# Cross-attention and a mixture-of-experts feed-forward on one core: setup and first turns reordered, biases added at read-out, feed-forward from the middle of turn 2

## The chip, the cores and the metric

One core of one Trainium2 chip runs the whole program. The metric is the device time of one execution, in microseconds (us), as the median of several runs. The engines are TensorE (PE in the profile; its weight loads are PEld), VectorE (DVE), ScalarE (ACT), GpSimd (POOL) and SyncE (SP), whose queue issues the DMAs.

## What is computed

`x`, `fside` (here `ctx1`) and `ctx_1024` (here `ctx2`) have the shape (16, 256, 256): 16 batches of 256 tokens of width 256. Everything is float32.

```
x1 = x + attention(layernorm(x), ctx1, memory = ctx2)
     q = ln(x) Wq + bq;  k = ctx1 Wk + bk;  v = ctx1 Wv + bv
     k, v = concat([k, ctx2]), concat([v, ctx2])        # 512 keys
     16 heads of 16;  softmax(q k^T / 4) v;  then Wp + bp
out = x1 + sum over 8 experts e of  cw_e * (silu(z Wg_e) * (z Wu_e)) Wd_e
     z = layernorm(x1);  F = 1024
     cw = softmax(z w_router) * softmax(10 z w_gating), normalised over e
```

## The kernel before, in words

Precision. A float32 operand is split into a high part (rounded to the fp32r format) and a low part (the rest), and a product is three matmuls: high x high, high x low, low x high (`passes`). The high part is written by ScalarE (or VectorE for the attention weights), the low part by VectorE (`h_lo`, `xT_lo`, `cT_lo`) or GpSimd (`wg_lo`, `kstack`, `qstack`).

Turns and steps. The order of work is written out by hand. One turn handles one batch's attention and has 32 steps; in step i the scores of item i+8 (`ps_s`, L714), their maximum (`negmax`, L1092, VectorE), the transposed scores (`ps_t`, L723), the exponential (`Pt`, L870, ScalarE), its low part (`Pt_lo`, L1039 on VectorE for i % 8 in 1, 3, 5, 7, else L1182 on GpSimd) and, six steps behind, the product with V (L694, L696) are done, each engine walking the same list of steps. Two turns ahead of turn 0 (-2 and -1) hold the setup of the first batches. `turn.has(d)` says whether batch b+d exists, and `turn.wait` waits on a counter.

The list `MISC` (L279) names further TensorE items by step: cT and xT (transposes of the context and of the normalised x), kv, q and o (projections; `project`, L504, q and o in two halves over two steps), kT (transposes of the key stack), qq (of the maxima and the query stack), aT, x2T, lg and cwT (transpose of the attention result, transpose of z, router logits, transpose of the combine weights), and y (output transposes of a finished group). ScalarE or VectorE reads each item's bank in the same step. Before the feed-forward the items, the scores and the transposed scores alternate between two PSUM banks; from then on each has one bank (`one_bank`, `bank`).

Biases. `project` begins with a matmul of `minus_one` by `brow` (L507), which puts the bias in PSUM; brow is made in the setup.

Feed-forward. A group is two batches (512 tokens), 8 experts, 8 steps each of 128 hidden columns: 64 steps a group, 512 in all, one for each attention step. A step f has six gate matmuls (L617, ps_s), six up matmuls (L617, ps_t) and six down matmuls (L651), each of 512 columns; ScalarE takes tanh (L737) and the high part (L742), VectorE the products L904 and L911 and the low part L916. At the last step of an expert VectorE weighs the output (two L931) and GpSimd adds it (L1140). It starts at turn `LAG` = 3, step 0; `before_ffn` and `first_weights` prepare the first step and the first weights in one piece, ahead of turn 3 and ahead of turn 1. Turns 3 to 15 are joint (attention and feed-forward); after turn 15's attention the rest of the feed-forward runs alone.

Setup. SP issues Wq, Wk, Wv, Wp, the router's two parts, four bias rows and the first three expert weights, and then X and C1 of batch 0 (L411, L414). VectorE waits for the first ten of these, splits all weights, clears tiles and makes brow; TensorE waits for all of it (`const_ready`, `w_split`) before its first instruction.

Of the kernel before, what the change touches and what calls it, by code (L numbers as in the profile page):

```python
# [21 lines left out]
ALU = mybir.AluOpType  # L22
# [14 lines left out]
def bass_xattn_moe_ffn_kernel(nc, x, ctx1, ctx2, Wq, bq, Wk, bk, Wv, bv, Wp, bp, w_router, w_gating,  # L37
# [28 lines left out]
    LAG = GB + 1  # L66
# [8 lines left out]
    FTURNS = FSTEPS // STEPS  # L75
    assert FTURNS == GB * GROUPS
# [12 lines left out]
    with ExitStack() as ctx:  # L89
# [11 lines left out]
        with ExitStack() as early:  # L101
            def raw(name, shape, dt=F32):
                return early.enter_context(nc.sbuf_tensor(name, shape, dt))

            wraw = raw("wraw", [P, 4, DC, D])
            rraw = raw("rraw", [P, DC, 2 * E])
            braw, bhi = raw("braw", [2, 4, D]), raw("bhi", [2, 4, D], F32R)
# [11 lines left out]
        brow = sb("brow", [P, 4, D], F32R)  # L119
        minus_one = sb("minus_one", [P, P], F32R)  # L120
# [6 lines left out]
        XN = sb("XN", [P, QT, D])  # L127
        C1 = sb("C1", [P, QT, D])
# [3 lines left out]
        QK = sb("QK", [P, QT, D])  # L132
        VF = sb("VF", [P, KC, D])
# [68 lines left out]
        w_in = sem("w_in"); const_ready = sem("const_ready"); w_split = sem("w_split")  # L202
        x_in = Count("x_in", 16); c1_in = Count("c1_in", 16); c2_in = Count("c2_in", 16)
        xr_in = Count("xr_in", 16)
# [8 lines left out]
        kv_ps = Count("kv_ps", 2); k_done = Count("k_done", 2); v_done = Count("v_done", 2)  # L213
# [24 lines left out]
        CONSTS = 13  # L238
        W_PARTS = 13
        LAST = LAG + FTURNS  # L240

        class Turn:


            def __init__(self, b):
                self.b, self.ffn = b, LAG <= b
                self.closed = (b - LAG) // GB - 1 if self.ffn and (b - LAG) % GB == 0 and b > LAG else None
# [22 lines left out]
        def turns(body, before_ffn=None, first_weights=None):  # L270

            for b in range(-2, LAST + 1):
                if b == 1 and first_weights:
                    first_weights()
                if b == LAG and before_ffn:
                    before_ffn()
                body(Turn(b))

        MISC = [(0, "kT", 5, 0), (1, "kT", 6, 0), (2, "qq", 1, 0), (3, "cT", 0, 1), (4, "kT", 7, 0), (5, "y", 0, 0),  # L279
# [9 lines left out]
        def released(turn, name, k, d):  # L289

            if name == "y":
                return [] if turn.closed is None else [(y_done, turn.closed * GB + k + 1)]
            if name == "qq":
                ahead, da = q_ahead(k, d)
                freed = [(d, qm_done, 2 * k + 2), (da, qT_done, 2 * ahead + 2)]
                return [(count.sem, (turn.b + at) * count.per + nth) for at, count, nth in freed if turn.has(at)]
            count, nth = {"kT": (kT_done, k + 1), "kv": (v_done, k + 1), "xT": (xT_l, 1), "cT": (cT_l, 1), "aT": (aT_l, 1),
                          "x2T": (x2T_l, 1), "q": (q_done, 1), "o": (x1_done, 1), "lg": (ldif_done, 1),
                          "cwT": (cwT_done, 1)}[name]
            return [(count.sem, (turn.b + d) * count.per + nth)] if turn.has(d) else []  # L300

        def misc(turn, step):

            for n, (s, name, k, d) in enumerate(MISC):
                if s == step and released(turn, name, k, d):
                    return n, name, k, d
            return None, None, None, None

        def second_half(turn, step):

            n, name, _, d = misc(turn, step - 1)
            return (n, name) if name in ("q", "o") else (None, None)

        def one_bank(turn, banks, i):

            return banks[0] if turn.ffn else banks[i % 2]

        def octet_bank(turn, o):

            return ps_a[:] if turn.ffn or o % 2 else ps_o[:, 0, :]  # L320

        def wait_read_out(eng, turn, count, d, i):

            turn.wait(eng, count, d, i if turn.ffn else i - 1)

        ORDER = [sum(item[1] != "y" for item in MISC[:n]) for n in range(len(MISC))]

        def bank(turn, n):

            return ps_o[:, 1, :] if ORDER[n] % 2 and not turn.ffn else ps_m[:]  # L330

        def wait_bank(eng, turn, n):

            same = [m for m in range(len(MISC)) if turn.ffn or MISC[m][1] != "y" and (ORDER[m] - ORDER[n]) % 2 == 0]
            earlier = [(Turn(turn.b - 1), m) for m in same] + [(turn, m) for m in same if m < n]
            for then, m in reversed(earlier):
                freed = released(then, *MISC[m][1:])
                for counter, value in freed:
                    eng.wait_ge(counter, value)
                if freed:  # L340
                    return
# [7 lines left out]
        V_AT = ((3, 5, 0), (0, 14, 1), (1, 22, 1), (2, 30, 1))  # L349
# [42 lines left out]
        def _(eng):  # L392
            for n, w in enumerate((Wq, Wk, Wv, Wp)):
# [848 lines left out]
```

## Time and profile before

| | |
|---|---|
| median of 3 runs | 2844.45 us (2843.43 to 2844.73) |
| profiled execution | 2842.41 us, span 2840.6 us |
| PE, PEld busy | 2754.5 us (97%), 2248.5 us (79%) |
| DVE, ACT, POOL busy | 2151.3 us (76%), 1702.8 us (60%), 1686.0 us (59%) |
| mean granted clock of TensorE | 0.989 |

"Busy" is the time in which at least one instruction of the engine runs; matmuls overlap in the pipeline, so the mean length of one is above the time from one to the next. The span runs from the first to the last instruction. A clock of 1.00 is 2.4 GHz, 0.50 is 1.2 GHz.

### The profile page before, as it was taken

What the parts mean: (1) busy time and instruction counts of PE and PEld (TensorE: products, weight loads), DVE (VectorE), ACT (ScalarE), POOL (GpSimd) and SP (SyncE); (2) the same over time, 40 slices, a digit from 0 to 9 for tenths busy, and PEclk for the clock granted to TensorE, in tenths of its full rate; (3) what the DMA queues carried; (4) which work ended last, traced back from release to release, by engine and by line L of the source; (5) the groups of instructions that cost most, each with busy time, mean ns of one, the idle gap of its engine ahead of it and who ended that gap; (6) DMA issues with size and microseconds to landing.
All of it is one profiled execution on the core that took longest, in us unless ns stands there. A gap on an engine that the chain in (4) does not pass through costs nothing.

```text
span 2840.6 us, 47444 instructions
## 1 busy us (share of the span) xinstructions
PE 2754.5 (97%) x16512; PEld 2248.5 (79%) x16512; DVE 2151.3 (76%) x3218; ACT 1702.8 (60%) x3313; POOL 1686.0 (59%) x1612
## 2 busy tenths in 40 slices
PE   5789999999999999999999999999999999999998
PEld 3567888888887888888888887888888888887887
DVE  4787787878878787787878778787787777766665
ACT  4776666666666666665666666666666665544443
POOL 2655666556666566666566666565666655554554
PEclk8899999999999999999999999999999999999999
DMA  1002232232322323232232322223222233333332
GB/s 56 31 20 86 82 97 86 79 112 86 98 89 83 104 86 94 90 97 94 75 101 93 102 88 84 92 90 105 82 90 86 79 108 91 102 105 112 104 103 83
DMA packets 250715, 251.76 MB, mean 89 GB/s; under 512 B 15848, under 2 KB 242288, under 8 KB 250480
## 3 DMA queue, kind: packets, MB, share of 16 engines
q1 hardware_dynamic: 250480, 248.73, 28.6%
q8 instruction: 135, 2.21, 0.3%
q14 instruction: 100, 0.82, 0.1%
HBM read 240.15 MB, written 8.52 MB: 88 GB/s over the span
## 4 chain that ended last, share of the span: by engine, by line
PE 86%; DVE 7%; ACT 3%; issue 3%; POOL 1%; SPq 0%; DMA 0%; POOLq 0%; ACTq 0%; DVEq 0%
PE ps_t L617 23%; PE ps_s L617 23%; PE ps_o L651 22%; PE ps_s L714 4%; PE ps_t L723 3%; PE ps_m L513 2%; PE ps_a L694 2%; PE ps_a L696 2%; DVE Pt_lo L1039 1%; PE ps_m L551 1%; DVE hf L911 1%; PE ps_m L521 1%; PE ps_m L558 1%; PE ps_m L566 1%; DVE css L973 1%
## 5 line engine op out<-in xcount | busy, mean ns | idle before, releaser
L916 DVE TENSOR_TENSOR h_lo<-hf,h_hi 128x512 fp32r<-128x512 f32 x512 | 545.5, 1065 | 323.0 <-ACT h_hi L742 317.6
L742 ACT ACTIVATE h_hi<-hf 128x512 fp32r<-128x512 f32 x512 | 323.5, 632 | 574.3 <-DVE hf L911 571.4
L904 DVE SCALAR_TENSOR_TENSOR hf<-hf,ps_s 128x512 f32<-128x512 f32 x512 | 349.8, 683 | 255.1 <-ACT hf L737 251.6
L1182 POOL TENSOR_TENSOR Pt_lo<-Pt 128x512 f16<-128x512 f32 x256 | 285.6, 1116 | 432.3 <-ACT Pt L870 431.4
L737 ACT ACTIVATE hf<-ps_s 128x512 f32<-128x512 f32 x512 | 306.2, 598 | 300.4 <-PE ps_s L617 161.1
L1121 POOL TENSOR_TENSOR wd_lo<-stage_w,wd_hi 128x512 fp32r<-128x512 f32 x256 | 338.1, 1321 | 139.5 <-ACT wd_hi L749 139.0
L1121 POOL TENSOR_TENSOR wg_lo<-stage_w,wg_hi 128x512 fp32r<-128x512 f32 x256 | 337.1, 1317 | 137.2 <-ACT wg_hi L749 137.2
L651 PE MATMUL ps_o<-h_hi,wd_hi 128*128 128x512 f32 x1024 | 399.4, 390 | 0.9 <-DVE h_lo L916 0.9
L651 PE MATMUL ps_o<-h_lo,wd_hi 128*128 128x512 f32 x1024 | 399.6, 390 | 0.0
L651 PE MATMUL ps_o<-h_hi,wd_lo 128*128 128x512 f32 x1024 | 398.7, 389 | 0.0
L1092 DVE TENSOR_REDUCE negmax<-ps_s 128x1 f32<-128x512 f32 x512 | 346.8, 680 | 31.4 <-PE ps_s L714 27.4
L911 DVE TENSOR_TENSOR hf<-hf,ps_t 128x512 f32<-128x512 f32 x512 | 347.3, 678 | 17.9 <-PE ps_t L617 1.0
L1121 POOL TENSOR_TENSOR wu_lo<-stage_w,wu_hi 128x512 fp32r<-128x512 f32 x256 | 359.8, 1405 | 0.0
L870 ACT ACTIVATE Pt<-ps_t 128x512 f32<-128x512 f32 x512 | 303.9, 595 | 59.4 <-PE ps_t L723 56.0
L617 PE MATMUL ps_t<-xh,wu_hi 128*128 128x512 f32 x1024 | 319.9, 393 | 5.3 <-DVE hf L911 5.2
L617 PE MATMUL ps_s<-xh,wg_hi 128*128 128x512 f32 x1024 | 322.3, 395 | 1.1 <-ACT Pt L870 0.9
L617 PE MATMUL ps_s<-xh,wg_lo 128*128 128x512 f32 x1024 | 318.3, 392 | 0.0
L617 PE MATMUL ps_s<-xl,wg_hi 128*128 128x512 f32 x1024 | 317.2, 391 | 0.0
L617 PE MATMUL ps_t<-xh,wu_lo 128*128 128x512 f32 x1024 | 316.8, 390 | 0.0
L617 PE MATMUL ps_t<-xl,wu_hi 128*128 128x512 f32 x1024 | 315.6, 389 | 0.0
L714 PE MATMUL ps_s<-KTs,QTs 128*128 128x512 f32 x512 | 236.7, 463 | 13.6 <-DVE negmax L1092 7.8
L1039 DVE TENSOR_TENSOR Pt_lo<-Pt 128x512 f16<-128x512 f32 x256 | 224.6, 877 | 15.2 <-ACT Pt L870 14.9
(189 smaller groups left out, 5121.7 us busy)
## 6 DMA issues: line engine op xcount, KB each, us to landing
stage_w<-in_L_ffn_w_gate_dram SPq DMA_DIRECT2D x256, 256.0 KB, 2.7
stage_w<-in_L_ffn_w_up_dram SPq DMA_DIRECT2D x256, 256.0 KB, 2.9
stage_w<-in_L_ffn_w_down_dram SPq DMA_DIRECT2D x256, 256.0 KB, 2.7
cwb<-d_cw SPq DMA_DIRECT2D x64, 256.0 KB, 3.5
X<-in_x_dram SPq DMA_DIRECT2D x32, 256.0 KB, 3.0
C<-in_fside_BxSxS_dram SPq DMA_DIRECT2D x16, 256.0 KB, 3.4
VF<-in_ctx_dram SPq DMA_DIRECT2D x16, 256.0 KB, 3.0
d_x<-X SPq DMA_DIRECT2D x16, 256.0 KB, 3.1
```

Source lines behind the costliest of these rows:

```text
L617: mm = pe.matmul(ps[:], wt[:, c, q * P:(q + 1) * P], tok[:, c].rearrange("p k n -> p (k n)"), start=(n == 0), stop=(n == 3 * DC - 1))
L651: mm = pe.matmul(ps_o[:, c, :], wt[:, q, c * P:(c + 1) * P], hid[:], start=(at == 0 and n == 0), stop=(at == EXPERT - 1 and n == 2))
L714: pe.matmul(one_bank(turn, ps_s, i)[:], QTs[:, h // 2 % QRING, h % 2, qt * P:(qt + 1) * P], KTs[:, h // 2, :], start=True, stop=True).then ...
L737: act.activation(hf[:], ps_g[:], ACT.Tanh, scale=0.5).then_inc(tanh_done, 1)
L742: act.activation(h_hi[f % FC][:], hf[:], ACT.Copy).then_inc(hh_done, 1)
L870: act.activation(Pt[i % RING][:], one_bank(turn, ps_t, i)[:], ACT.Exp).then_inc(exp_done.sem, 1)
L904: dve.scalar_tensor_tensor(out=hf[:], in0=hf[:], scalar=1.0, in1=ps_g[:], op0=ALU.add, op1=ALU.mult).then_inc(gate_done, 1)
L911: dve.tensor_tensor(hf[:], hf[:], ps_u[:], ALU.mult).then_inc(hf_done, 1)
L916: dve.tensor_tensor(h_lo[f % FC][:], hf[:], h_hi[f % FC][:].bitcast(F32), ALU.subtract).then_inc(hl_done, 1)
L1092: dve.tensor_reduce(negmax[:, (i // 4) % 2, i % 4:i % 4 + 1], one_bank(turn, ps_s, i)[:], AX.X, ALU.max, negate=True).then_inc(max_done.se ...
L1121: pool.tensor_tensor(lo[:], raw_weights(n), hi[:].bitcast(F32), ALU.subtract).then_inc(wl_done, 1)
L1182: pool.tensor_tensor(Pt_lo[slot][:], Pt[slot][:], Pt[slot][:].bitcast(BF16)[:, 1::2], ALU.subtract).then_inc(lo_pool.sem, 1)
```

## The change

What it does, part by part:

- The feed-forward starts at step `START` = 83, counted from turn 0: turn 2, step 19. `closed`, the one-bank rule, the octet banks and `before_ffn` follow that step instead of the turn.
- Setup: X and C1 of batch 0 are loaded first, then Wk, Wv, Wq, the four biases (each to all 128 partitions), the memory half of VF, Wp, the router's parts and the first expert weights. The weights' high parts go to ScalarE and are made, like the low ones, at given steps of the turns -2 and -1. Clears of qstack, QTs and mq move from VectorE to GpSimd. TensorE waits for what each item needs and no longer for everything.
- Turn -1 has its own steps for cT, kv, xT and q.
- Biases: L507 goes. VectorE reads key and value with their biases in one operation per half (into `KVM`), q with its scaled bias into `QF`; GpSimd adds bp to X1.
- q and o are projected in one step. aT, o, x2T, lg, cwT, y and the norm of X1 with its router work change steps; z has a tile of its own (`X2`).
- The first expert weights are split one at a time over turns 1 and 2.
- `keep_busy`: 66 transposes of `ident` into `ps_a` in the turns -2 and -1, which nobody reads.

```diff
+    START = GB * STEPS + 19
+    CLOSED = START // STEPS + GB
...
-                f = (self.b - LAG) * STEPS + step
+                f = self.b * STEPS + step - START
...
+        ITEMS = [(0, "kT", 5, 0), (1, "kT", 6, 0), (2, "qq", 1, 0), (3, "cT", 0, 1), (4, "kT", 7, 0), (5, "aT", 0, -1),
+                 (6, "qq", 2, 0), (8, "o", 0, -1), (9, "kv", 0, 1), (10, "qq", 3, 0), (11, "kv", 1, 1), (13, "xT", 0, 1),
+                 (14, "qq", 4, 0), (15, "x2T", 0, -1), (16, "q", 0, 1), (17, "lg", 0, -1), (18, "qq", 5, 0), (19, "kT", 0, 1),
+                 (20, "kT", 1, 1), (21, "cwT", 0, -1), (22, "qq", 6, 0), (23, "y", 0, 0), (24, "y", 1, 0), (25, "kT", 2, 1),
+                 (26, "qq", 7, 0), (27, "kT", 3, 1), (28, "kT", 4, 1), (30, "qq", 0, 1)]
+
+        FIRST_AT = {"cT": (1,), "kv": (3, 7), "xT": (5,), "q": (9,)}
...
+        HIGH_AT = {(-2, 9): (0, 1), (-1, 4): (2,), (-1, 16): (3, 4)}
+        LOW_AT = {(-2, 27): (0, 1), (-1, 4): (2,), (-1, 16): (3, 4)}
+        EARLY_WEIGHTS = {(1, 4): (0, 0), (1, 12): (1, 0), (1, 20): (2, 0), (2, 1): (0, 1), (2, 9): (1, 1)}
...
-        V_AT = ((3, 5, 0), (0, 14, 1), (1, 22, 1), (2, 30, 1))
+        V_AT = ((3, 5, 0), (0, 15, 1), (1, 21, 1), (2, 29, 1))
...
+                for n, w in enumerate((Wk, Wv, Wq, Wp)):
+                    if n == 3:
+                        for m, v in enumerate((bq, bk, bv, bp)):
+                            eng.dma_start(bias[:, m], v.rearrange("(o n) -> o n", o=1).broadcast_to([P, D])).then_inc(b_in, 16)
+                        eng.dma_start(VF[:, QT:KC, :], one(c2_v, Turn(-1), 1)).then_inc(c2_in.sem, 16)
+                    eng.dma_start(wraw[:, n], w.rearrange("(c p) n -> p c n", p=P)).then_inc(w_in[n], 16)
...
-                pe.matmul(ps[:, col:col + width], minus_one[:], brow[:, bias].rearrange("p b n -> p (b n)"),
-                              start=True, stop=False)
...
+            KEEP_BUSY = {(-2, 0): 14, (-1, 2): 10, (-1, 4): 6, (-1, 6): 6, (-1, 8): 6, (-1, 12): 24}
...
+                for _ in range(n):
+                    pe.transpose(ps_a[:, 0:P], ident[:], ident[:])
...
+                    for t in range(QT):
+                        mm = project(ps, t * D, D, (xT_hi, xT_lo), t, (wq_hi, wq_lo))
+                    mm.then_inc(q_ps.sem, 1)
...
-            pe.wait_ge(const_ready, CONSTS)
-            pe.wait_ge(w_split, W_PARTS)
...
-                        act.activation(QK[:, k, :], ps[:, 0:D], ACT.Copy).then_inc(k_done.sem, 1)
-                        act.activation(VF[:, k, :], ps[:, D:2 * D], ACT.Copy).then_inc(v_done.sem, 1)
...
-                        norm_stats(turn, -1, 15, step, X1, x1_done, st2, mv2, ve2, st2_done, mv2_done, ve2_done, rstd2_done)
+                        norm_stats(turn, -1, 9, step, X1, x1_done, st2, mv2, ve2, st2_done, mv2_done, ve2_done, rstd2_done)
...
+                        dve.tensor_tensor(KVM[:, k:k + QT + 1:QT, :], ps[:].rearrange("p (s n) -> p s n", n=D), bias[:, 1:3, :],
+                                          ALU.add).then_inc(kv_done.sem, 1)
...
+                        dve.scalar_tensor_tensor(out=QF[:], in0=ps[:].rearrange("p (t n) -> p t n", n=D), scalar=SCALE,
+                                                 in1=bias[:, 0:1, :].broadcast_to([P, QT, D]),
+                                                 op0=ALU.mult, op1=ALU.add).then_inc(q_done.sem, 1)
...
+                    if step == 4 and turn.has(-1):
+                        turn.wait(pool, xr_in, -1, 16)
+                        pool.wait_ge(b_in, 16 * 4)
+                        pool.tensor_tensor(X1[:], X1[:], bias[:, 3:4, :].broadcast_to([P, QT, D]),
+                                           ALU.add).then_inc(xb_done.sem, 1)
```

## Rows read from the trace of the kernel before

**Rows 1.** Stretches: length, busy us (instructions) of each engine, clock, DMA share, GB/s.
```profile
core 0: us, PE busy (x) PEld busy (x) DVE busy (x) ACT busy (x) POOL busy (x), PEclk, DMA share, GB/s
21.30:51.50 30.20, 20.27 (x76) 14.45 (x77) 8.49 (x20) 13.83 (x29) 9.19 (x14) 0.68 0.12 35
51.50:202.20 150.70, 116.82 (x1129) 89.43 (x1128) 112.58 (x214) 111.67 (x244) 90.13 (x116) 0.89 0.09 28
202.20:223.80 21.60, 15.81 (x158) 10.95 (x157) 18.97 (x45) 17.11 (x40) 13.85 (x19) 0.92 0.01 2
402.90:573.00 170.10, 169.44 (x1029) 139.06 (x1029) 134.71 (x200) 105.97 (x209) 106.68 (x102) 1.00 0.30 91
2577.20:2618.00 40.80, 40.80 (x183) 33.19 (x183) 26.34 (x34) 20.11 (x35) 19.21 (x15) 1.00 0.41 123
```

**Rows 2.** Timeline of the setup: start us, us, engine, line, operation, idle before and releaser.
```profile
7.12 0.68 DVE L879 CAST bhi<-braw 2x1024 fp32r<-2x1024 f32 x1 [7.12 <-DMA braw<-in_L_xattn_bp_dram]
...
17.62 1.12 PE L521 MATMUL ps_o<-ident,C 128*128 128x128 f32 x4 [17.62 <-DVE mq L898]
21.35 0.77 PE L507 MATMUL ps_o<-brow,minus_one 128*128 128x512 f32 x1 [2.61 <-DVE cT_lo L1051]
21.91 1.05 PE L513 MATMUL ps_o<-wkv_hi,cT_hi 128*128 128x512 f32 x2
25.77 0.63 PE L513 MATMUL ps_o<-wkv_hi,cT_hi 128*128 128x512 f32 x2
27.16 0.60 PE L521 MATMUL ps_m<-ident,XN 128*128 128x128 f32 x4
39.09 1.27 POOL L1194 TENSOR_TENSOR qstack<-QK,qstack 128x512 fp32r<-128x512 f32 x1 [5.73 <-ACT qstack L781]
40.51 0.46 PE L566 MATMUL ps_m<-ident_r,qstack 128*128 128x128 f32 x2 [0.21 <-POOL qstack L1194]
51.53 0.60 ACT L870 ACTIVATE Pt<-ps_t 128x512 f32<-128x512 f32 x1 [0.38 <-PE ps_t L723]
```

**Rows 3.** The exponentials of the first 202.3 us: count, min/median/max ns, first and last start.
```profile
L870 ACT ACTIVATE Pt<-ps_t x83: 570/599/644, 51.5 to 201.5; 128x512 f32<-128x512 f32 x83
```

**Rows 4.** Timeline where the feed-forward begins.
```profile
223.17 0.57 ACT L870 ACTIVATE Pt<-ps_t 128x512 f32<-128x512 f32 x1
223.84 0.70 PE L617 MATMUL ps_s<-xh,wg_hi 128*128 128x512 f32 x2 [0.94 <-ACT Pt L870]
```

**Rows 5.** Exponentials of turn 4; then the exponentials of turn 5's step 19 and turn 6's step 0.
```profile
L870 ACT ACTIVATE Pt<-ps_t x33: 571/594/604, 402.9 to 573.0; 128x512 f32<-128x512 f32 x33
...
675.27 0.59 ACT L870 ACTIVATE Pt<-ps_t 128x512 f32<-128x512 f32 x1
743.95 0.59 ACT L870 ACTIVATE Pt<-ps_t 128x512 f32<-128x512 f32 x1
```

**Rows 6.** Timeline of the end: the first gate matmuls of two steps running.
```profile
2820.76 0.61 PE L617 MATMUL ps_s<-xh,wg_hi 128*128 128x512 f32 x2
2824.84 0.61 PE L617 MATMUL ps_s<-xh,wg_hi 128*128 128x512 f32 x2
```

**Rows 7.** The bias line's matmuls into the one bank ps_m, by shape.
```profile
L507 PE MATMUL ps_m<-brow,minus_one x80: 276/276/388, 129.2 to 2491.2; 128*128 128x256 f32 x56, 128*128 128x512 f32 x24
```

**Rows 8.** Waits between 51.5 and 202.2 us: us in total, times, longest.
```profile
PE ps_o L507 <- DVE xT_lo L1051: 9.8, 3, 3.8
PE ps_m L558 <- POOL mq L1166: 4.2, 1, 4.2
```

**Rows 9.** Waits of TensorE from 240 to 2400 us; then VectorE's groups of turn 4.
```profile
PE ps_t L617 <- DVE hf L911: 3.7, 10, 0.4
...
L1039 DVE TENSOR_TENSOR Pt_lo<-Pt 128x512 f16<-128x512 f32 x16 | 14.5, 908 | 0.0
L931 DVE SCALAR_TENSOR_TENSOR wout<-ps_o,cwb 128x512 f32<-128x512 f32 x8 | 5.4, 681 | 0.0
L973 DVE SCALAR_TENSOR_TENSOR css<-lsum 128x2 f32<-128x2 f32 x1 | 1.3, 1268 | 0.0
```

More of the change, by code:

```diff
@@ L314, in one_bank @@
[L314 to L341, printed above, removed]
+            return [(count.sem, (b + d) * count.per + nth)] if turn.has(d) else []
@@ new lines, in items_of @@
+        def items_of(b):
+            present = [(s, name, k, d) for s, name, k, d in ITEMS if released(b, name, k, d)]
+            if b == -1:
+                present = [(FIRST_AT[name][k] if name in FIRST_AT else s, name, k, d) for s, name, k, d in present]
+            return sorted(present)
+        items, last_in = {}, {}
+        for b in range(-2, LAST + 1):
+            for step, name, k, d in items_of(b):
+                joint = b * STEPS + step >= START
+                one = joint or len(items) % 2 == 0
+                items[b, step] = (name, k, d, one, last_in.get(one, []))
+                last_in[one] = released(b, name, k, d)
+                if not joint:
+                    last_early = dict(last_in)
@@ new lines, in misc, with bank, wait_all, score_bank @@
+        def misc(turn, step):
+            return items.get((turn.b, step), (None, None, None, None, None))
+        def bank(one):
+            return ps_m[:] if one else ps_o[:, 1, :]
+        def wait_all(eng, freed):
+            for counter, value in freed:
+                eng.wait_ge(counter, value)
+        def score_bank(j):
+            return ps_s[0] if j - AHEAD >= START else ps_s[j % 2]
+        def wait_scores_read(eng, j):
+            wait_for(eng, max_done.sem, j if j - AHEAD >= START else j - 1)
@@ new lines, in key_bank, with wait_keys_read, octet_in_a, octet_bank @@
+        def key_bank(j):
+            return ps_t[0] if j >= START else ps_t[j % 2]
+        def wait_keys_read(eng, j):
+            wait_for(eng, exp_done.sem, j if j >= START else j - 1)
+        def octet_in_a(o):
+            return o % 2 == 1 or o * OCT + OCT + 3 >= START
+        def octet_bank(o):
+            return ps_a[:] if octet_in_a(o) else ps_o[:, 0, :]
+        def octet_before(o):
+            return next((m for m in range(o - 1, -1, -1) if octet_in_a(m) == octet_in_a(o)), -1)
@@ L811, in body @@
                         high_of(f + 1)
-                    n, name, k, d = misc(turn, step)
-                    ps = bank(turn, n) if name else None
+                    name, k, d, one, _ = misc(turn, step)
+                    ps = bank(one) if name else None
                     if name in ("xT", "cT", "aT", "x2T"):
@@ L1040, in body @@
                                           ALU.subtract).then_inc(lo_dve.sem, 1)
-                    n, name, k, d = misc(turn, step)
-                    ps = bank(turn, n) if name else None
+                    name, k, d, one, _ = misc(turn, step)
+                    ps = bank(one) if name else None
                     if name in ("xT", "cT", "aT", "x2T"):
```

353 lines of the change are left out of this document (173 added, 180 removed), and 4 rows, old and new, of the table MISC.

## The prediction

> **What bounds the kernel now.** I read three views in this order: the table of stretches, the waits, then single rows for the lengths.
>
> The table of stretches [rows 1] splits the run. From 223.8 us on, when the feed-forward begins, TensorE is busy for 169.4 of the 170.1 us of a turn, at the full clock, and for all of 40.8 us in the stretch without attention. VectorE, ScalarE and GpSimd have 21%, 38% and 37% of the turn free. So from there on the time is a sum of matmul issues. Before it TensorE is busy for 20.3 of 30.2 us (clock 0.68) and 116.8 of 150.7 us (clock 0.89). There the time is a chain of small hand-overs between four engines, and none of them is full. A change can win in two ways: drop matmuls from the full part, or reach it sooner.
>
> **The base.** The profiled execution took 2842.4 us: a span of 2840.6 and 1.8 around it. The median of the runs shown is 2844.45, 2.0 above it. I count in the span and add 3.8.
>
> Lengths I need:
> - A feed-forward step alone is 4.08 us (2820.76 to 2824.84, [rows 6]), 18 matmuls of 512 columns, 0.227 us each.
> - A joint turn is 170.1 us (402.9 to 573.0, 33 exponentials, so 32 steps, [rows 5]). Its last 13 steps (19 to 31) take 743.95 - 675.27 = 68.7 us, of which 13 x 4.08 = 53.0 are feed-forward. The attention part of 13 such steps costs TensorE 15.6 us.
> - Exponential 0 starts at 51.5 and exponential 82, the 83rd, at 201.5 [rows 3]. Exponential 95 starts at 223.17 and the first gate matmul follows at 223.84, 0.67 later [rows 4]. The new kernel lets the first gate matmul wait for exponential 82 in the same way. With nothing else changed it would start at 201.54 + 0.67 = 202.2.
> - From the first gate matmul to the end: 2840.6 - 223.8 = 2616.8 us.
>
> **Part 1, feed-forward from step 83.** It starts 223.8 - 202.2 = 21.6 us earlier. The 13 attention steps that it then runs beside are now charged in the full part: +15.6. Net -6.0. The feed-forward steps after the attention fall from 96 to 83 and are in this sum (512 steps at 4.08 either way).
>
> **Part 2, biases at read-out.** L507 goes. Of its 96 matmuls, 80 write ps_m: 24 of 512 columns and 56 of 256 [rows 7]. In the full part are the 24, and of the 56 all but the 4 of the first two batches' output projections: 52. A 512-column one holds TensorE for 0.227 us as above, one of 256 for half of it, by my estimate. 24 x 0.227 + 52 x 0.113 = 5.4 + 5.9 = 11.3 us, all on the path (9 to 13 if the short one costs 0.07 to 0.15). What replaces it: VectorE reads out key/value (two reads) and q (one) with the bias, at 0.68 us for such a read (L931, [rows 9]): +2.0 us a turn, and ScalarE loses about as much. GpSimd adds one 128x512 operation a turn (1.27, [rows 2]). In the full part VectorE has 35 us of a turn free and GpSimd 63, so I charge nothing, unless the steps pile up (below).
>
> **Part 3, the setup.** Now X and C1 are the 14th and 15th transfers issued. VectorE starts only once the tenth has landed (7.12), splits everything, clears tiles, and TensorE's first transpose is at 17.62 and the first projection at 21.35 [rows 2]. In the new order X, C1, Wk and Wv go first. By the same queue four such transfers have landed by about 7.1; the weight splits (0.6 each on ScalarE as its 128x512 row at 51.53, 0.68 on VectorE as at L931), the normalisation of X, which waits for GpSimd's longer row of clears, and the low half of cT come before the projection. I put it at 9.4 us: 12 earlier. The clears with which VectorE now ends its setup (mq releases the row at 17.62) go to GpSimd, before its first rstd; there they could hold XN, and with it cT_lo, by up to 3 us (QTs has four times 512 columns, at 0.68 each).
> From the projection to the first q transpose there are 19.2 us now (40.51), and 11.0 more to the first exponential (51.53). The new order puts xT before the second key/value projection, the memory half of kstack before everything, and q two hand-overs earlier. Counting each hand-over once by its present duration I reach the q transpose 12 to 13 us after the projection at the full clock. Bounds: nothing gained after the projection, 12 us in all; everything gained and the 11 us cut to 9.5, 20 us. I take 17, nearer the upper end because the present 19.2 us hold idle time of TensorE (10 of 30.2 us in [rows 1]).
> The added transposes: 66, each 0.28 us at the half clock (four in 1.12, 17.62) or 0.15 at the full one (four in 0.60, 27.16), the pipeline's end included [rows 2]: at most 18.5 and 9.9 us. 42 of them stand ahead of waits for transfers, read-outs and splits and are hidden; the last 24 stand between q and the first key transpose, where GpSimd's low halves of kstack and qstack (1.27 each, 39.09) take over 2 us anyway. At the full clock they cost 0 to 1, at the half clock 2 to 5.
> Do they hold the clock? The trace has the full clock after a dense row of projections (25.77: two in 0.63, where 21.35 and its followers took 1.05) but only 0.68 as the mean of the 30.2 us [rows 1], in which the later part is sparse, transposes mostly; it does not separate the kinds. The Trainium skill (TensorE: Matmul & The Clock Gate, Part 4: PE-mode transpose) says that the full rate "doesn't engage" for transpose mode, which doesn't count as busy in the same way. This trace neither shows nor excludes it. By that rule the fillers would buy nothing and rival A would be the result.
>
> **Part 4, the attention-only turns.** 150 us now, 82 steps. In the waits [rows 8]: 9.8 us of TensorE's q projection on xT_lo, since q stands one step after xT; it becomes three steps. I take half, 5, because ScalarE and VectorE then hold it up elsewhere. 4.2 us once, on mq, which stood behind the three weight splits that GpSimd does in one lump ahead of turn 1; they are spread over turns 1 and 2: 3. The bias matmuls of the first batches: 2. Against it two more weight splits and the bias sum on GpSimd (1.3 us each), and aT, x2T and the norm moved closer to what feeds them: -3. Sum 7. From below: -5 (each of the closer steps a new wait of 2 us in turns 1 and 2). From above 15 (all 14 us of the waits and a denser TensorE).
>
> **Part 5, order inside the joint turn.** TensorE waits there 0.7 us a turn (170.1 less 169.4, [rows 1]), with hf named ten times for 3.7 us in all [rows 9]: VectorE is late once a turn. The expert's read-out (two L931, 0.68 each) moves from odd steps to 2, 10, 18 and 26, where VectorE also does a Pt_lo (0.91). Step 10 becomes 6.7 us of VectorE, step 19 6.8, step 20 6.6, against 5.32 a step; small operations take up to 1.27 (css) [rows 9]. (Counted as 3.4 for an odd step's four feed-forward and score operations, 3.9 for an even one's five, and what is put there: two L931, statistics, read-outs and small operations.) The new overruns are 2.0 at 10 and 11 and 2.8 at 19 and 20, each followed by light steps. I leave the wait as it is. SP gets one new order too: the combine weights' store (step 22) and their load stand ahead of the next weight loads in its queue; the load of the combine weights is due four steps, 21 us, later, and a weight transfer has its own step of slack, so nothing is charged. Bounds: all gone, -8; 1 us more a turn, +13.
>
> **Sum.** 2840.6 - 6.0 - 11.3 - 17 - 7 = 2799.3 of span; +3.8 = 2803 us.
>
> **Rivals.**
> A. The fillers don't lift the clock and stand before the key transposes. Part 3 gives 12, part 4 gives 4: 2803 + 5 + 3 = 2811. For it: the clock of 0.68 in the setup; against it: the projections alone should lift it.
> B. New waits in the joint turn, where in-order VectorE is late at steps 10 and 20: 1 us a turn, 13.4 turns, 2816. For it: TensorE already waits once a turn with VectorE at 134.7 of 170.1 us.
> C. Slower: VectorE becomes the bound where read-out, Pt_lo and small operations meet (steps 2, 10, 18, 26 and 20). Each place would have to cost 1 us net, four a turn, 54 us: 2857. It decides from 3.1 us a turn on (41.7 / 13.4 to be level). Against it: 35 us free in a turn, and light odd steps behind each place.
> D. The early turns gain all their waits and the joint wait disappears: 2803 - 8 - 4 = 2791.
> E. No change: the early stretch gives nothing (24 back) and B costs 1.3 a turn: 2844. That would be the change not doing what it says.
>
> **How the numbers follow.** Forecast 0.60 (own range 2795 to 2810), A 0.14, B 0.10, D 0.10, C 0.03, E 0.03. The range 2789 to 2818 holds the forecast, A, most of B and D. Within 0.2% (5.7 us, what a measurement can tell here) means 2838.8 to 2850.1: 0.03. Faster 0.94, slower 0.03.
>
> **What would show it.** First projection near 9.4 and first exponential near 34.5 us; first gate matmul near 178; no bias matmul; joint turn 169.3 (170.1 less 0.9); first exponential later than 39 speaks for A, together with 0.5 in the clock before it; joint turns over 170.1 for B, over 172.3 for C. I am wrong if a joint turn grows, or if the 83 steps take as long as now.

## The result: faster, by a third of what was forecast, with the profile after

The changed kernel takes 2829.18 us (median of 5, 2824.51 to 2832.13) against 2844.45 (5 runs, 2840.74 to 2845.57): a ratio of 0.995 [0.9939, 0.9961], 15 us. The forecast was 2803, its range 2789 to 2818. The direction was right and the size was not. The profiled execution is the fastest of the five, 2824.51 us with a span of 2822.3, so it stands 4.7 us below the median.

First the stretches of the changed kernel, in the columns of [rows 1]: setup, the attention-only turns, one joint turn, the whole joint part.

```profile
core 0: us, PE busy (x) PEld busy (x) DVE busy (x) ACT busy (x) POOL busy (x), PEclk, DMA share, GB/s
0.00:33.70 33.70, 25.69 (x144) 22.21 (x144) 21.19 (x41) 16.32 (x32) 15.11 (x28) 0.85 0.40 117
33.70:174.40 140.70, 110.14 (x1113) 82.48 (x1111) 122.75 (x225) 109.12 (x235) 97.72 (x124) 0.93 0.11 33
402.00:573.40 171.40, 170.02 (x1033) 139.41 (x1032) 136.88 (x205) 104.36 (x202) 106.50 (x101) 1.00 0.31 95
240.00:2400.00 2160.00, 2137.53 (x12897) 1750.67 (x12895) 1726.32 (x2541) 1314.26 (x2541) 1347.06 (x1270) 1.00 0.29 91
```

Against [rows 1] the early stretches are shorter (setup 33.7 us where 51.5 stood, attention alone 140.7 where 150.7 stood). The joint turn is longer though its bias matmuls are gone, and in it TensorE is idle for 1.4 us instead of 0.7. The exponentials say the same, by count, shortest/median/longest in ns, first and last start; they answer [rows 3, 5]. The first 83, then 353, which are 11 joint turns:

```profile
L907 ACT ACTIVATE Pt<-ps_t x83: 577/598/632, 33.7 to 173.9; 128x512 f32<-128x512 f32 x83
L907 ACT ACTIVATE Pt<-ps_t x353: 571/598/604, 423.4 to 2309.6; 128x512 f32<-128x512 f32 x177
```

82 steps now take 140.2 us (150.0 before). A joint turn takes (2309.6 - 423.4) / 11 = 171.5 us; the same count of the kernel before (402.9 to 2275.8) gives 170.3. I had forecast 169.3. The timeline (columns of [rows 2]) has the first projection and the first gate matmul, forecast at 9.4 and 178:

```profile
9.38 0.71 PE L536 MATMUL ps_o<-wkv_hi,cT_hi 128*128 128x512 f32 x2 [2.05 <-DVE cT_lo L1082]
...
174.55 1.19 PE L657 MATMUL ps_s<-xh,wg_hi 128*128 128x512 f32 x2 [3.17 <-issue]
```

So up to the first gate matmul the kernel is 3.5 us ahead of the forecast. From there to the end it takes 2822.3 - 174.55 = 2647.7 us, where the forecast had 2799.3 - 178 = 2621.3. That stretch is 26.4 us too long; less the 3.5 gained before it, the span misses its forecast by 23.0 us (2822.3 against 2799.3) and the median by 26. All of the miss lies behind the first gate matmul.

The waits of the changed kernel between 240 and 2400 us (us in total, times, longest) show what is new; they answer [rows 9]:

```profile
DVE h_lo L942 <- ACT h_hi L780: 284.2, 366, 3.1
...
POOL qstack L1235 <- ACT qstack L828: 86.0, 12, 7.2
...
ACT qstack L828 <- PE ps_m L609: 28.1, 12, 2.3
...
PE ps_t L657 <- DVE hf L937: 17.2, 14, 2.0
...
PE ps_s L751 <- DVE negmax L1131: 4.3, 12, 0.4
```

TensorE's wait for hf went from 3.7 us [rows 9] to 17.2. Two further waits come exactly once a turn (12 times): ScalarE's qstack waits 2.3 us for TensorE's transposes, and GpSimd's waits 7.2 us for ScalarE's. One such place is steps 18 and 19 of turn 4. The lines below are the timeline of 516 to 529 us, engine by engine: TensorE, ScalarE, GpSimd, VectorE.

```profile
...
520.41 0.33 PE L609 MATMUL ps_m<-ident_r,qstack 128*128 128x128 f32 x2
...
523.88 0.50 PE L691 MATMUL ps_o<-h_hi,wd_hi 128*128 128x512 f32 x1
524.22 0.39 PE L691 MATMUL ps_o<-h_hi,wd_lo 128*128 128x512 f32 x1
...
517.87 0.62 ACT L787 ACTIVATE wu_hi<-stage_w 128x512 fp32r<-128x512 f32 x1
520.84 1.06 ACT L828 ACTIVATE qstack<-QF 128x1024 fp32r<-128x1024 f32 x1 [2.35 <-PE ps_m L609]
521.80 0.30 ACT L855 ACTIVATE lexp<-ldif 128x16 f32<-128x16 f32 x2
522.01 0.61 ACT L780 ACTIVATE h_hi<-hf 128x512 fp32r<-128x512 f32 x1
...
521.98 1.31 POOL L1235 TENSOR_TENSOR qstack<-QF,qstack 128x512 fp32r<-128x512 f32 x1 [7.17 <-ACT qstack L828]
523.24 1.75 POOL L1163 TENSOR_TENSOR wg_lo<-stage_w,wg_hi 128x512 fp32r<-128x512 f32 x1
524.94 1.73 POOL L1163 TENSOR_TENSOR wu_lo<-stage_w,wu_hi 128x512 fp32r<-128x512 f32 x1
...
518.90 0.69 DVE L957 SCALAR_TENSOR_TENSOR wout<-ps_o,cwb 128x512 f32<-128x512 f32 x1
522.66 1.17 DVE L942 TENSOR_TENSOR h_lo<-hf,h_hi 128x512 fp32r<-128x512 f32 x1 [3.06 <-ACT h_hi L780]
...
526.75 1.20 DVE L995 TENSOR_TENSOR cprod<-lexp 128x16 f32<-128x16 f32 x1
...
528.65 0.64 DVE L937 TENSOR_TENSOR hf<-hf,ps_t 128x512 f32<-128x512 f32 x1
```

How to read it. hf was ready at 518.98 (L937, 0.69 from 518.29), but h_hi starts only at 522.01: on ScalarE it stands behind qstack, and qstack may overwrite its tile only when TensorE has transposed the last of its eight pairs (L609, 520.41; the list's item "qq", 5), which the list puts late in this same step 18. VectorE's h_lo waits 3.06 us for h_hi, with the read-out, the Pt_lo and the rest of the step behind it. In step 19 the router's operations (L994 to L1001) and the octet's read-out stand ahead of hf, so hf comes at 528.65, and TensorE stands idle for 0.93 us until 529.44. GpSimd stands still for 7.17 us and then has two weight splits to make up.

The cause that this points to, tested below, is one number in a line of the diff that neither my prediction nor my shortened diff has: `self.qs_at, self.ks_at, self.ms_at = (10, 8, 2) if b == -1 else (18, 12, 13)`. qs_at is the step in which both engines split the next query stack. The old code had ScalarE's half at step 19 and GpSimd's at 20.

The wait also costs clock, though not each time. In turn 3 TensorE is idle for 2.02 us from 355.6 on, until the hf of step 19 is there, and a stretch at 0.50, 1.2 GHz, follows. These are three consecutive stretches (columns of [rows 1]):

```profile
350.00:358.30 8.30, 5.92 (x27) 4.04 (x26) 7.60 (x13) 3.67 (x9) 8.30 (x7) 1.00 0.21 64
358.30:361.70 3.40, 3.40 (x10) 2.62 (x9) 3.24 (x5) 2.46 (x5) 1.98 (x5) 0.50 0.23 77
361.70:370.00 8.30, 8.30 (x41) 6.74 (x41) 6.71 (x12) 4.95 (x11) 4.25 (x4) 1.00 0.21 66
```

The same happens at 703.1, in turn 5. Each costs 1.7 us, half of 3.4. The same gap stands in turns 7 and 12, and there the clock stays at 1.00; in the other eight of the twelve turns it is 0.93 to 0.95 us long:

```profile
1045.83 0.47 PE L657 MATMUL ps_t<-xh,wu_hi 128*128 128x512 f32 x1 [2.04 <-DVE hf L937]
1901.69 0.47 PE L657 MATMUL ps_t<-xh,wu_hi 128*128 128x512 f32 x1 [2.03 <-DVE hf L937]
```

Over the joint part TensorE's idle time rose from 12.9 to 30.9 us (all of its gaps after 240 us). 18 + 3.4 of the missing time is thereby found. Part of the rest is in matmuls after a late input, as the one at 523.88, followed after 0.34 us instead of 0.227: a record is 0.39 us long, so the idle column doesn't show a wait that is shorter than the overlap. These were not added up.

### The profile page after: what moved, and what is told of

It reads as the page before. It is cut to its first block, busy times and chain, and to the rows that moved or that the text cites. A ratio compares the mean times of both kernels' runs of the same rounds, so it can differ in the third digit from the quotient of the medians.

```text
span 2822.3 us, 47420 instructions
## 1 busy us (share of the span) xinstructions
PE 2748.6 (97%) x16482; PEld 2242.9 (79%) x16482; DVE 2206.9 (78%) x3255; ACT 1679.4 (60%) x3238; POOL 1719.8 (61%) x1631
## 4 chain that ended last, share of the span: by engine, by line
PE 81%; DVE 9%; issue 5%; ACT 4%; POOL 0%; DMA 0%; SPq 0%; ACTq 0%; POOLq 0%; DVEq 0%
PE ps_s L657 22%; PE ps_t L657 22%; PE ps_o L691 21%; PE ps_s L751 4%; PE ps_t L761 3%; PE ps_m L536 3%; PE ps_a L733 1%; DVE Pt_lo L1070 1%; DVE negmax L1131 1%; PE ps_a L735 1%; ACT h_hi L780 1%; DVE hf L937 1%; PE ps_m L594 1%; DVE X L1014 1%; DVE hf L930 1%
## 5 line engine op out<-in xcount | busy, mean ns | idle before, releaser
L942 DVE TENSOR_TENSOR h_lo<-hf,h_hi 128x512 fp32r<-128x512 f32 x512 | 558.2, 1090 | 355.2 <-ACT h_hi L780 350.6
L1163 POOL TENSOR_TENSOR wg_lo<-stage_w,wg_hi 128x512 fp32r<-128x512 f32 x256 | 343.0, 1340 | 331.9 <-ACT wg_hi L787 329.1
L937 DVE TENSOR_TENSOR hf<-hf,ps_t 128x512 f32<-128x512 f32 x512 | 347.4, 679 | 21.6 <-DVE hf L930 0.7
L1163 POOL TENSOR_TENSOR wu_lo<-stage_w,wu_hi 128x512 fp32r<-128x512 f32 x256 | 350.0, 1367 | 0.0
L1070 DVE TENSOR_TENSOR Pt_lo<-Pt 128x512 f16<-128x512 f32 x256 | 249.8, 976 | 6.5 <-ACT Pt L907 6.5
```

What stands on the lines that cost most here:

```text
L937: dve.tensor_tensor(hf[:], hf[:], ps_u[:], ALU.mult).then_inc(hf_done, 1)
L942: dve.tensor_tensor(h_lo[f % FC][:], hf[:], h_hi[f % FC][:].bitcast(F32), ALU.subtract).then_inc(hl_done, 1)
L1163: pool.tensor_tensor(lo[:], raw_weights(n), hi[:].bitcast(F32), ALU.subtract).then_inc(wl_done, 1)
```

## Experiments

T1 in the expectations is the theory just told, that qs_at is the cause. The rivals are named where they come. "After" is the changed kernel and all ratios are to the kernel before.

**1. Undo the one number.**

```diff
-                self.qs_at, self.ks_at, self.ms_at = (10, 8, 2) if b == -1 else (18, 12, 13)
+                self.qs_at, self.ks_at, self.ms_at = (10, 8, 2) if b == -1 else (19, 12, 13)
```

> The changed kernel with one number altered: the split of q into qstack stands at step 19 (ScalarE and GpSimd) again instead of 18. Theory T1 (ScalarE waits at step 18 for the qq transposes that TensorE issues late in the same step, with the high part of h queued behind): ScalarE's wait of 2.3 us for ps_m ahead of qstack goes, the joint turn falls from 171.7 to about 169.5 us, median 2803 to 2809 us. Rival T2 (VectorE is overfull at steps 18 to 20 by the expert's read-out and the router's small operations): the joint turn stays at 171 or more, median 2824 to 2832.

Measured: 2791.1 us, 0.982 [0.9807, 0.9833]. It is 38 us faster than the changed kernel by the medians and 31.6 by the profiled executions (spans of 2790.7 and 2822.3), and 12 us faster than the lower end of T1's range. First e1's 83 and 353 exponentials, then its step 19 in the timeline (VectorE's h_lo and hf, at the place shown above):

```profile
L907 ACT ACTIVATE Pt<-ps_t x83: 573/599/631, 35.2 to 171.6; 128x512 f32<-128x512 f32 x83
L907 ACT ACTIVATE Pt<-ps_t x353: 570/598/604, 417.4 to 2279.0; 128x512 f32<-128x512 f32 x177
```

```profile
518.94 0.15 DVE L998 SCALAR_TENSOR_TENSOR css<-lsum 128x2 f32<-128x2 f32 x1
...
519.72 0.64 DVE L937 TENSOR_TENSOR hf<-hf,ps_t 128x512 f32<-128x512 f32 x1
521.06 1.06 DVE L942 TENSOR_TENSOR h_lo<-hf,h_hi 128x512 fp32r<-128x512 f32 x1 [0.70 <-ACT h_hi L780]
```

The turn is 169.2 us, the forecast's 169.3. h_lo waits 0.70 for h_hi, both qstack waits are gone, TensorE's wait for hf is 4.1 us, and its idle time after 240 us 12.8. From 240 us on no half-clock stretch is left but the last 3 us of the run. T1 holds in the direction and in the turn; its price was larger than T1 said.

**2. The same number in the old kernel.** ScalarE's half from step 19 to 18 (`if step == 19 and turn.has(1)` becomes 18), and later both halves at 18.

> The kernel before with that one number altered the other way: ScalarE's split of q into qstack at step 18 instead of 19 (GpSimd's stays at 20). T1: the same wait appears in the old order, the joint turn grows from 170.5 by 1 to 2.5 us, median 2860 to 2880. T2: nothing happens, since VectorE's order is the old one, 2843 to 2847.

> The kernel before with both halves of q's split at step 18, ScalarE's (as in e2) and GpSimd's. T6: the cost that e2 did not show appears, 1 us or more a turn over e2's, 2856 to 2872. T5: as e2, 2843 to 2848.

Measured: 2844.44, 1.0005 [0.9996, 1.0014], and 2849.93, 1.0029 [1.0017, 1.0041]. The first misses T1's number and is in T2's range; the second is in neither of its ranges, 2 us above T5's. The timeline of the first on ScalarE does show the wait, and h_hi behind it:

```profile
499.35 1.06 ACT L781 ACTIVATE qstack<-QK 128x1024 fp32r<-128x1024 f32 x1 [1.96 <-PE ps_m L566]
500.31 0.61 ACT L742 ACTIVATE h_hi<-hf 128x512 fp32r<-128x512 f32 x1
```

In the old order 2 us of ScalarE's waiting cost nothing that the medians can tell; by the exponentials its joint turn is 0.3 us longer (170.57 against 170.27), 4 us in the run. GpSimd's wait adds 5.5 us by the medians (6.8 by the ratios, the two runs having been made beside different runs of the kernel before). In the new order both together cost 38. So the wait is the cause only together with what stands around it, and the next runs look for the partner.

**3. The router's small operations** on VectorE at steps 19 and 20: `router_weights(turn, step)` is called ahead of the hidden product; here it is called after h_lo and the read-out. e5 does this to the changed kernel, e6 to e1.

```diff
-                    router_weights(turn, step)
...
                     if f is not None and f % EXPERT == EXPERT - 1:
                         weigh_output(f, 1)
+                    router_weights(turn, step)
```

> The changed kernel, ScalarE's split of q left at step 18, but VectorE does the router's small operations of steps 19 and 20 after h_lo instead of between its two hf products. Theory T3 (the wait on ScalarE costs only because these small operations, lengthened to 1.2 and 1.3 us, then stand ahead of the late hf): the joint turn falls from 171.7 to 170.2 us or less, median 2800 to 2812. Rival T1 as first stated (the wait costs by itself, 2.3 us with h_hi behind it): the joint turn stays at 171.2 or more, median 2822 to 2832.

> e1 with the router's small operations after h_lo. What is left of TensorE's waits for hf at step 20 (0.4 us a turn in e1) goes: 2 to 6 us faster than e1, 2785 to 2789. If negmax becomes late instead (it now stands behind them), as fast as e1 or slower, 2790 to 2797.

Measured: e5 2815.57, 0.9906 [0.9889, 0.9922], a median outside both theories' ranges, 14 us under the changed kernel (9.7 by the spans). But its joint turn did not fall: 171.57 us, the side of T1 and not of T3.

```profile
L907 ACT ACTIVATE Pt<-ps_t x353: 569/597/602, 417.0 to 2304.2; 128x512 f32<-128x512 f32 x177
```

What e5 gained lies outside these 11 turns (82 steps in 136.6 us instead of 140.2, and the end of the run). And e5 less e6, the price of step 18 with the router's operations late in their steps, is 33.8 us: that they stand ahead of hf is hardly the point.

e6 2781.82, 0.9786 [0.9772, 0.9801], is faster than it was expected to be, 61 us under the kernel before and 47 under the changed one. Of the kernels that leave nothing out only e11 below, e6 with more unread transposes, is as fast. The joint part of e6 and its 11 turns (168.8 us each):

```profile
240.00:2400.00 2160.00, 2158.93 (x13103) 1779.70 (x13102) 1755.37 (x2582) 1333.98 (x2577) 1376.68 (x1289) 1.00 0.30 92
```

```profile
L907 ACT ACTIVATE Pt<-ps_t x353: 570/597/602, 415.0 to 2271.8; 128x512 f32<-128x512 f32 x177
```

TensorE is idle 1.07 of 2160 us, where it was idle 5.2 in e1. Of the 9 us between e1 and e6 some 7 lie between exponentials 96 and 511: TensorE's wait for an hf that stands behind the router's operations. The kernel before has such a wait too ([rows 9]; at 557.8 it is 0.38 us), and I left it as it was.

Leaving the router's seven operations out altogether, with ScalarE's and GpSimd's halves at step 18 (e15) and 19 (e16). These two kernels leave the router's weights out of the output (the combine weights are a constant 0.125), and ScalarE's lexp loses its two waits for VectorE with them:

> The changed kernel (q's split at step 18) without the router's seven small operations on VectorE at steps 19 and 20; the combine weights are a constant 0.125, so the router's weights are left out of the output. To be read against e16. Theory T7 (ScalarE's wait delays h_hi by about 3 us, and what makes it dear is that steps 19 and 20 leave VectorE no room to catch up; without the router's operations it can): the run is at most 10 us slower than e16. Rival T5 (the wait costs TensorE its price whatever stands on VectorE): 25 us or more slower than e16.

> e1 (q's split at step 19) without the same seven operations. What TensorE still waits for hf at step 20 goes: as fast as e6 or up to 4 us faster, 2777 to 2784.

Measured: 2797.36, 0.9843 [0.983, 0.9857], and 2778.48, 0.9775 [0.9762, 0.9789]. e16 came as expected, e15 between its theories' ranges. Without the router step 18 costs 18.9 us, with it 38 (or 33.8 where the operations stand late): nearly half of the price hangs on the presence of these operations, not on their place in the step.

**4. The read-out of an expert.** It falls on steps 2, 10, 18 and 26 because the feed-forward starts at step 19. START moves it: +20 instead of +19 (e4, odd steps); +23 (steps 6, 14, 22, 30) with step 18 (e9) and step 19 (e10). For +23 and for the next experiment's +27 the output transposes y move to steps 27 and 28, kT 2 to 4 to 23 to 25, the output's store to 28 and 30.

> e1 with the feed-forward one step later (84 instead of 83), so that the expert's read-out falls on odd steps, where VectorE has no Pt_lo. By the count of work 0.5 us slower than e1. If the collisions on even steps cost time (T2, or rival B of the prediction): the joint turn is 0.5 us or more shorter than e1's and the run 4 to 10 us faster.

> The changed kernel with ScalarE's split of q at step 18 as it has it, but the feed-forward from step 87 and y at 27 and 28 (kT 2 to 4 at 23 to 25), so that the expert's read-out falls on steps 6, 14, 22 and 30 and no longer on the step with the wait. To be read against e10. Theory T4 (the wait is dear only where VectorE's read-out of the expert and the router follow it; in the old order it cost 0.3 us a turn): the joint turn is at most 0.7 us longer than e10's, the run at most 9 us slower than e10. Rival T5 (ScalarE's own work in that step, two weight splits, the exponentials of the router and the split of q, makes the wait dear wherever the read-out is): 2 us or more a turn, 25 us or more slower than e10.

> e9 with the split of q at step 19. Against e8 (the same with the feed-forward from 91): by the count of work 1.8 us faster, and faster still by what read-out at steps 2, 10, 18, 26 costs there: 2796 to 2801. If the steps 6, 14, 22, 30 are worse places, over 2803.

Measured: e4 2839.75, 0.999 [0.9981, 0.9998]; e9 2830.88, 0.9965 [0.9951, 0.9978]; e10 2799.89, 0.9854 [0.9841, 0.9868]. e9 less e10 is 31 us (T5's side; T4 said at most 9): the read-out need not be in the step of the wait. e10 came as expected. And e4, which was expected within some us of e1, is 48 us slower with the feed-forward one step later. In its step 11 VectorE has the read-out, the key/value read-out, the norm's small operations (1.3 us each) and a long h_lo: from one negmax to the next (471.52 to 480.98) 9.5 us go by, 8.6 of them busy, against the 5.3 of a step. Its joint turn is 172.8 us, and these are TensorE's waits from 240 to 2400 us:

```profile
PE ps_s L751 <- DVE negmax L1131: 9.2, 25, 0.5
PE ps_t L657 <- DVE hf L937: 8.3, 13, 0.7
PE ps_o L691 <- DVE h_lo L942: 5.5, 15, 0.9
```

By the starts of TensorE's matmuls 2.4 of the 3.6 us that a turn is longer than e1's fall on steps 11 to 13. That fits the mechanism of rivals B and C, at a place that the change avoids; e1's fullest stretch, at step 10, is 8.05 us long and costs nothing that shows.

**5. GpSimd's half alone** back at step 20, with ScalarE's at 18 (e12) and, in e6, with ScalarE's at 19 (e14):

```diff
-                    if step == turn.qs_at and turn.has(1):
+                    if step == (10 if turn.b == -1 else 20) and turn.has(1):
```

> The changed kernel with ScalarE's split of q still at step 18, but GpSimd's low half of it (which waits for ScalarE's) at step 20, as in the old order. Theory T6 (GpSimd stands 7.2 us in that wait with two weight splits behind it, which then run beside VectorE's h_lo and Pt_lo and finish late): the joint turn falls from 171.7 to 170.0 us or less, median 2794 to 2808. Rival T5 (ScalarE's own wait is what costs): the joint turn stays at 171 or more, median 2820 to 2832.

> e6 (ScalarE's split of q at 19, the router's small operations after h_lo) with GpSimd's half at step 20 instead of 19. T6: GpSimd waits at 19 for ScalarE's half too, but with one weight split behind it and the partner early in its step, so 0 to 3 us faster than e6, 2779 to 2782. T5: within 1 us of e6.

Measured: 2823.12, 0.9935 [0.9923, 0.9948], and 2785.75, 0.9802 [0.9789, 0.9816]. The first is in T5's range, not in T6's: GpSimd's 7.2 us wait is worth at most 6 of the 38 (3.2 by the spans, and the joint turn stays at 171.55), though no single wait of the list is longer. In e6 the later step costs 4 us (the first 82 steps take 138.6 instead of 136.2), where I had expected a small gain.

**6. All partners away at once**: no router operations, read-out on other steps (+23), GpSimd's half at step 20; ScalarE's at 18 (e17) or 19 (e18). Both leave the router's weights out of the output, as e15 and e16 do.

> e15 with, besides, the expert's read-out off step 18 (feed-forward from 87, y at 27 and 28 as in e9) and GpSimd's half of q's split at step 20: ScalarE's wait at step 18 with nothing extra behind it on VectorE and GpSimd, as in the old order. The router's weights are left out of the output as in e15. To be read against e18. If the price of the wait is the sum of what stands behind it (router, read-out, GpSimd's half): at most 6 us slower than e18, as e2 was 1. If the wait has a price of its own in the new order: 12 us or more slower than e18.

> e17 with q's split at step 19 on ScalarE, as its control; the router's weights are left out as there. By e16 plus the four later steps: 2780 to 2790 us.

Measured: 2803.93, 0.9862 [0.9846, 0.9879], and 2789.81, 0.9814 [0.98, 0.9829]. ScalarE's wait alone still costs 14.1 us (14.8 by the spans), 1.2 in a joint turn where it was 0.3 in the old order (experiment 2). e17's and e18's exponentials, 170.6 and 169.3 us a turn:

```profile
L905 ACT ACTIVATE Pt<-ps_t x353: 569/597/602, 404.5 to 2280.7; 128x512 f32<-128x512 f32 x177
L905 ACT ACTIVATE Pt<-ps_t x353: 569/597/602, 403.2 to 2265.9; 128x512 f32<-128x512 f32 x177
```

TensorE's idle time after 240 us is only 2.5 us larger in e17 (10.3 and 7.8). The 1.2 us show in the starts of its matmuls: step by step they fall back between steps 19 and 22, by 0.27, 0.75 and 0.21 us.

**7. The terms of the sum, measured.** e3 is e1 without the unread transposes (`KEEP_BUSY = {}`); e11 is e6 with 30 instead of 10 of them at turn -1, step 2. e7 is e1 with a matmul nobody reads where each bias matmul stood. e8 is e1 with the feed-forward 8 steps later.

```diff
+                pe.matmul(ps[:, col:col + width], ident_r[:], wkv_hi[:, 0, 0:width], start=True, stop=True)
```

> e1 without the 66 transposes that nobody reads. If they hold TensorE's clock: the clock is at 0.5 for 10 us or more of the setup, the first exponential starts at 36 to 40 us instead of 33.7 and the run is 3 to 6 us slower than e1. If transposes do nothing for the clock (the rule weighed in the prediction): the first exponential within 1 us of 33.7, the run within 1 us of e1 or faster.

> e6 with 30 instead of 10 unread transposes ahead of the first key/value projection, so that TensorE has no gap of more than 1 us there. If the clock at the first projections is what the setup's length hangs on: first exponential at 32 to 33 us instead of 34.0, 1 to 2 us faster than e6. If the setup is a chain of the other engines: first exponential within 0.7 us of 34.0 and the run within 1.5 us of e6.

> e1 with one more matmul of the projection's width ahead of each projection, as the bias matmul was; nobody reads what it writes. By the prediction's part 2: 11.3 us in the full part and 0 to 3 before it, 2802 to 2806. If such matmuls hide in TensorE's slack: within 2 us of e1.

> e1 with the feed-forward 8 steps later (91), so that the expert's read-out falls on the same steps of a turn (2, 10, 18, 26), and y at 27 and 28 with kT 2 to 4 at 23 to 25. By the prediction's part 1 a step costs 1.66 us alone and 1.20 beside the feed-forward: 8 x 0.46 = 3.7 us slower than e1, 2794 to 2796. If the start does not matter: within 1 us of e1. If the phase of 8 was not what made e4 slow: 10 us or more slower than e1.

Measured: e3 2792.78, 0.9825 [0.9811, 0.9838]; e11 2781.3, 0.9787 [0.9774, 0.9801]; e7 2803.74, 0.9863 [0.9849, 0.9878]; e8 2801.95, 0.9857 [0.9842, 0.9871].
- Fillers: nothing that can be told, in either kernel (1.7 and 0.5 us between the medians). First exponential 35.2 with them, 34.3 without.
- Bias matmuls: 12.6 us by the medians, 10.3 by the spans, for all of them (forecast 11.3 in the full part and 2 before it).
- 8 steps later: 10.9 us by the medians, 9.3 by the spans (by part 1, 8 x (21.6 - 15.6) / 13 = 3.7). Its joint turn is 169.67, 0.43 longer than e1's, all of it at steps 28 and 29, so exponentials 96 to 511 take 5.1 us longer (2191.6 against 2186.5). Of the 9.3 that leaves 4.2 for the later start itself.

The fillers do change the clock. e1's stretches of the setup (columns of [rows 1]):

```profile
3.00:6.00 3.00, 3.00 (x17) 3.00 (x16) 2.82 (x9) 0.00 (x0) 2.62 (x5) 1.00 0.88 262
6.00:10.00 4.00, 0.92 (x9) 0.68 (x7) 2.34 (x5) 1.75 (x3) 0.71 (x1) 0.92 0.75 151
10.00:16.00 6.00, 5.61 (x20) 4.98 (x21) 1.79 (x4) 2.12 (x3) 1.04 (x1) 0.50 0.90 272
16.00:22.00 6.00, 6.00 (x49) 5.68 (x48) 2.78 (x4) 2.39 (x4) 1.67 (x3) 0.99 0.20 65
```

and e1's TensorE in the timeline:

```profile
1.53 3.25 PE L549 MATMUL ps_a<-ident 128*128 128x128 f32 x14 [1.53 <-POOL ident L1141]
4.57 1.06 PE L554 MATMUL ps_m<-ident,C 128*128 128x128 f32 x4
5.42 1.50 PE L549 MATMUL ps_a<-ident 128*128 128x128 f32 x10
10.39 1.19 PE L536 MATMUL ps_o<-wkv_hi,cT_hi 128*128 128x512 f32 x2 [3.47 <-DVE cT_lo L1082]
...
16.25 0.71 PE L536 MATMUL ps_o<-wkv_hi,cT_hi 128*128 128x512 f32 x2
```

14 transposes from 1.53 take 3.25 us (0.213 from one start to the next), the next ten, from 5.42, only 1.50 (0.109 from 5.995 on): the clock rose to full with nothing but transposes behind it. The clock column doesn't show the rise, it says 1.00 from 0 on in every run, also in e3, where the first projection runs at half speed; up to the first drop on record the distances have to be read. Then TensorE idles 3.47 us waiting for cT_lo, the records have the low level from 9.3 us on, and the first projection runs at half speed all the same. In e3 the q projection starts at 17.25 us and in e1 at 18.30. In e11 and e6 the first projections run at full speed (two matmuls in 0.71 and 0.63 us), and the first exponential comes at 33.6 and 34.0, at most 1.6 us ahead of e1 and e3. So the setup is mostly a chain of hand-overs, which a faster TensorE hardly shortens.

## Why the prediction was right and wrong

**Part 1, feed-forward from step 83: right** in sign, and in size as far as it was measured. e8 tests the rule for 8 steps: 4.2 us where the rule gives 3.7, once the longer turns are taken off. e8 as a whole (10.9) was outside its expected 2794 to 2796. The 6.0 for all 13 steps was not measured by itself.

**Part 2, bias matmuls: right.** 11.3 forecast, and 2 in part 4 for those before the full part; 10.3 to 12.6 measured for all of them. The VectorE read-outs that replace them were rightly charged nothing: e1's turn is 169.2 for 169.3.

**Part 3, setup: right.** First projection 9.38 us for 9.4, first exponential 33.7 for 34.5. "Do they hold the clock?" was the wrong question: they lift it, and it is worth nothing. Against the Trainium skill (TensorE: Matmul & The Clock Gate, Part 4: PE-mode transpose), on whose rule transposes don't engage the full rate, e1 has the full level from transposes alone (0.109 us apart instead of 0.213). Rival A's premise was false. Its price, fillers that hold up the key transposes at the half clock, was not measured; the first exponential at 33.7 and not later than 39 rules A out for this kernel.

**Part 4, attention-only turns: right in sign, too small.** 7 us forecast; 150.0 to 140.2 in the changed kernel and to 136.4 in e1, so 9.8 and 13.6. Nearly all of what I gave as the upper end (15) came. Step 18 costs here too, but not evenly: 3.8 us between after and e1, 0.4 between e5 and e6.

**Part 5, order inside the joint turn: this step failed.** I wrote "I leave the wait as it is" and counted only VectorE's work per step, and even there I named the right steps, 19 and 20. Two things were missed. First, the move of qstack from 19/20 to 18, which adds a wait to ScalarE behind transposes of its own step, with h_hi behind it. The bound of +13 for part 5 was made for VectorE alone; measured were 2.2 us a turn above e1 (171.48 against 169.24), 31.6 us between the profiled executions and 38 between the medians. Second, the interplay: h_lo comes 3 us late at step 18, ahead of steps 19 and 20, which the prediction itself counted among the fullest (6.8 and 6.6 against 5.32), and where the router's operations stand. Rival B had the place (step 20) and the sign, and 2816 of it was the nearest number, but its mechanism is not the one: with the same VectorE order and qstack at 19, e1 gives 2791.

With qs_at at 19 the sum closes. 2840.6 less 16.3 (first exponential at 35.2), 13.6 (82 steps), 12.6 (bias) and 6.0 (part 1) is 2792.1; e1's span is 2790.7. Two of the terms are soft: the 6.0 is the forecast's own, and the 12.6 holds the bias matmuls of the first turns, which are in the 13.6 too. e1's 2791 is rival D's number as well, but D's mechanism, the joint wait gone, is that of e6.

**How far the cause is settled.** Shown: qs_at makes the 38 us (experiment 1). About half of it needs the router's operations in steps 19 and 20, wherever they stand in the step (experiment 3), up to 6 us come by way of GpSimd (experiment 5), and 14 stay with ScalarE's wait when all three partners are taken away (experiment 6). These were measured in different kernels and need not add. Open: why ScalarE's wait is 1.2 us a turn there and 0.3 in the old order. The changed kernel has one thing more between qstack and h_hi on ScalarE (lexp, 0.30) and splits other weights in that step (wg and wu, where the old order has wd), but neither was tried by itself.

**"What would show it"** worked in part: "I am wrong if a joint turn grows" is what happened. The turn of 171.5 was also the sign named for B ("joint turns over 170.1"), and B's cause was not the one: the sign doesn't tell a late VectorE from a late ScalarE.

## What to carry to other kernels

When a change moves an instruction in an in-order list, look up what it waits for and where the list puts that: a consumer in the same step as a late producer stops its engine, and all that stands behind it. What that costs depends on the work around it: here 38 us in one order and 1 to 8 in the other. Read the whole diff for such numbers, not only the long parts; the smallest edit was worth more than twice the whole gain. And the longest single wait (GpSimd's 7.2 us, 86 in all) was worth at most 6 us, while TensorE's of 17 us in all was the one to follow back.

## What the runs showed of the hardware

- In an otherwise full stretch TensorE's clock fell for 3.4 us after a gap of 2.0 us at two places of the changed kernel (358.3 and 703.1 us), at a cost of 1.7 us each. After two more gaps of the same length (ended at 1045.8 and 1901.7) it did not, nor after any of the gaps of 1.35 us or less between 240 and 2800 us.
- Transposes alone lifted TensorE to the full rate (e1, above). A float32 transpose of 128x128 came every 0.21 us at 1.2 GHz and every 0.11 at 2.4.
- The same VectorE operation has two lengths. In the changed kernel h_lo (128x512) took 0.69 us at 515.72, when GpSimd had nothing to do, and 1.17 at 522.66, beside GpSimd's splits; css with two elements a partition took 0.15 and at other times 1.31. Over the whole run, the 170 h_lo beside which GpSimd did nothing took 0.69 to 0.70 us each, the other 342 between 0.69 and 1.83 (median 1.34); wout, which reads one operand from PSUM, stayed at 0.67 to 0.69 in all 112, 85 of them beside GpSimd's work. So the length goes with GpSimd's work; no run changed that by itself.
